# A PSUM bank chosen for every product, and new orders of all engines, in an attention and slot-mixture kernel

## The chip, the cores and the metric

The kernel runs on one core of a Trainium2 chip. Five engines work side by side, each through its own queue of instructions in order: TensorE (PE; its weight loads are shown as PEld), VectorE (DVE), ScalarE (ACT), GpSimd (POOL) and SyncE (SP, which here only starts transfers). They wait for each other by semaphores. Time is device time of one execution in microseconds (us), from several runs.

## What is computed

The input x has 32 batches of 256 tokens with 128 features. Each batch goes through two layers, each with a layer norm on both sides and a residual. Cut to what matters (16 heads of 8 features; 8 experts of 64 slots, so 512 slots; 512 hidden features):

```python
def _L0_attn_ref(x, ...):                   # a sum over the sequence in place of a softmax
    q = exp(x @ Wq.T + bq); k = exp(x @ Wk.T + bk); v = x @ Wv.T + bv     # per head
    kv = cumsum(k[:, :, :, None] * v[:, :, None, :], axis=1)
    num = einsum('zsD,zsDd->zsd', q, kv)
    den = sum(q * cumsum(k, axis=1), axis=-1)
    return (num / den) @ Wo.T + bo
def _L0_ffn_ref(x, ...):                    # soft mixture over slots
    xn, se = rms_norm(x, gamma_x), rms_norm(slot_embeds, gamma_slot)
    logits = einsum('bsd,etd->bset', xn, se)
    slots = einsum('bsd,bset->betd', xn, softmax(logits, axis=1))         # over the tokens
    processed = gelu(slots @ w1) @ w2
    return einsum('bnd,bsn->bsd', processed, softmax(logits, over all slots))
x = x + layernorm(attn(layernorm(x)))
x = x + layernorm(ffn(layernorm(x)))
```

## The kernel before

All weights stay in SBUF. A batch's 256 tokens are two per partition (c = 0 and 1), and all 32 batches go through one software pipeline: a `step(s)` of each engine's queue works on several batches at once, at different depths. Most operations are small functions, such as `gather_slots(n)`, and each engine's order of calls is written out by hand: `first_steps()` for the first batches, then `step(s)` in a loop, then `last_steps()`. Nothing else sets the order of the work.

The way of one batch n is this. DVE takes statistics of x (`x_statistics`), POOL raises the variance to the power -1/2 (`x_rstd_of`), DVE normalises (`x_normalise`, result xh), PE transposes (`x_transpose`), ACT and DVE make a high and a low part of it (`xT_high`, `xT_low`). `project(n, c)` gives q, k and v of one token parity; ACT evicts them to E (`qk_evict` with exp, `v_evict`). SP shifts E's odd tokens by one partition with a transfer (`shift_odd`, into prev). POOL forms outer products of k and v (`outer_even`, `outer_odd`, 1,024 columns each), adds them (`pair_sum`) and splits the sum (`sums_high` writes kv_hi, `sums_low` writes kv_lo). PE sums over partitions with a triangle (`cumulate(n, k)`, three thirds k), DVE multiplies each third with q (`multiply(n, k)`), reduces (`attention_sums`) and divides (`attention`). PE transposes att, ACT copies it (`attT_copy`), and `attention_out` gives y. ACT squares y, POOL gives its inverse root (`y_rstd_of`, y_rs), and DVE adds y to x (`first_residual`, x1).

Then the mixture: ACT squares x1, POOL gives x1_rs (`x1_rstd_of`), DVE normalises (`x1_normalise`, xn), PE transposes, ACT and DVE split. `logits(n)` fills the two banks of LB. DVE takes two maxima (`slot_maxima`, `part_maxima`), ACT takes four exponentials (`dispatch_exp`, disp_t), and DVE scales them (`dispatch_scale`). PE transposes disp_t (`dispatch_transpose`), ACT copies each half to disp (`dispatch_copy`), and PE gathers the slots (`gather_slots`). Their high and low parts are slT_hi and slT_lo. `hidden(n, f)` makes the four quarters of the hidden layer, ACT takes the Gelu of each, `process(n, h)` multiplies by w2, and `mixture(n)` mixes with comb. ACT squares the result, POOL gives o_rs, and DVE adds it to x1 (`second_residual`, res), which SP stores. ACT loads one table for Exp and one for Gelu in each step.

A product with both operands split is three matmuls (`three`). PSUM has eight banks of 512 columns. They are named in pairs: WB serves the projections, all transposes of x, att, xn and the maxima, the cumulative sums, y, and the attention sums ND; LA the dispatch transposes and the mixture; HB the gathered slots, the hidden quarters (f % 2) and process; LB the logits. At the start PE also runs matmuls with no use (`spin`), 130 in all, in places where it would wait.

Of the kernel before, what the change touches and what calls it, by code (L numbers as in the profile page):

```python
# [5 lines left out]
def attention_and_slot_mixture(  # L6
# [45 lines left out]
    with ctx:  # L52
# [6 lines left out]
        def sem(name):  # L59
# [97 lines left out]
        s_wT, s_woT, s_wop, s_wu, s_sesum, s_senorm, s_kappa = (  # L157
            sem("s_" + n) for n in ("wT", "woT", "wop", "wu", "sesum", "senorm", "kappa"))
        s_gxs, s_sefloor, s_sehi, s_wqkvhi, s_wqkv, s_w1hi, s_wo_t = (
            sem("s_" + n) for n in ("gxs", "sefloor", "sehi", "wqkvhi", "wqkv", "w1hi", "wo_t"))  # L160
        s_w2 = sem("s_w2")
# [14 lines left out]
        xT_lo_ready, qk_exp, kv_even, kv_odd, kv_den, kv_built = (  # L176
            sem("s_" + n) for n in ("xTlo", "qkexp", "kve", "kvo", "kvd", "kv"))
        kv_hi_ready, kv_lo_ready, qk_own_ready, own_den, own_ready, own_added = (
            sem("s_" + n) for n in ("kvhi", "kvlo", "qkown", "ownden", "own", "ownadd"))
        summed, den_ready, att_ready, att_T, attT_ready, wo_done = (  # L180
            sem("s_" + n) for n in ("summed", "deninv", "att", "attTp", "attT", "wo"))
        y_var, y_rstd, x1_ready, x1_var, x1_floor, x1_rstd = (
            sem("s_" + n) for n in ("yve", "yrs", "x1", "x1ve", "x1fl", "x1rs"))
        xn_ready, xnT_done, xnT_hi_ready, xnT_lo_ready, lb_done, part_ready = (
            sem("s_" + n) for n in ("xn", "xnT", "xnThi", "xnTlo", "lb", "part"))
# [34 lines left out]
        def _(sp):  # L220
# [9 lines left out]
            @each_batch  # L230
            def shift_odd(n):
                sp.wait_ge(qk_exp, n + 1)
# [19 lines left out]
            def step(s):  # L252
                load(s)
                store(s - 8)
                shift_odd(s - 1)
# [8 lines left out]
        def _(pool):  # L264
# [17 lines left out]
            def x_rstd_of(n):  # L282
                pool.wait_ge(x_stats, n + 1)
                if n == 2:
                    after(pool, xh_ready, n - 1)
# [9 lines left out]
            def wo_order():  # L295
                pool.wait_ge(s_woload, 16)
                pool.tensor_copy(wo_p[:, :].rearrange("p (d h) -> p d h", d=HD),
                                 w_in[:, 3, :].rearrange("p (h d) -> p d h", d=HD)).then_inc(s_wop, 1)

            def slot_norms():  # L300
                pool.wait_ge(s_sesum, 1)
# [6 lines left out]
            def sums_high(n):  # L308
                after(pool, cum_done[2], n - 1)
                if n == 1:  # L310
                    pool.wait_ge(kv_den, n + 1)
# [10 lines left out]
            def own_value(n):  # L322
                pool.wait_ge(own_den, n + 1)
# [30 lines left out]
            def outer_even(n):  # L354
                if n == 0:
                    pool.wait_ge(qk_exp, n + 1)
# [13 lines left out]
            @each_batch  # L370
            def pair_keys(n):
                u = n % 2
                pool.tensor_tensor(kv[:, KVF:FEAT], E[u][:, 0, DIM:2 * DIM], prev[u][:, 0:DIM], ALU.add)\
                    .then_inc(kv_den, 1)
# [10 lines left out]
            def first_steps():  # L385
                wo_order()
                slot_norms()
# [4 lines left out]
                outer_odd(1)  # L392
                outer_even(1)
                pair_sum(1)
                x_negative(1)
                pair_keys(1)
                own_value(0)
                sums_high(1)
                sums_low(1)
                own_product(1)  # L400
                x_rstd_of(3)
                y_rstd_of(0)
                outer_odd(2)
                x1_rstd_of(0)
                x_negative(2)
                own_value(1)
                outer_even(2)
                pair_keys(2)
                pair_sum(2)
                own_product(2)  # L410
                sums_high(2)
                sums_low(2)
                y_rstd_of(1)
                x_rstd_of(4)
                outer_odd(3)
                x1_rstd_of(1)
                x_negative(4)
                x_negative(3)
                own_value(2)
                outer_even(3)  # L420
                pair_keys(3)
                pair_sum(3)
                own_product(3)
                sums_high(3)
                x_rstd_of(5)
                sums_low(3)
                y_rstd_of(2)
                outer_odd(4)
                x1_rstd_of(2)
                own_value(3)  # L430
                outer_even(4)
                pair_keys(4)
                pair_sum(4)
                own_product(4)
                sums_high(4)
                x_rstd_of(6)
# [1139 lines left out]
```

## Time and profile before

| | us |
|---|---|
| median of 3 runs (lowest to highest) | 620.16 (617.2 to 620.59) |
| the profiled execution | 618.45 |
| its span, from the first instruction to the last | 616.7 |
| PE, PEld busy | 586.3, 498.7 |
| DVE, ACT, POOL busy | 488.9, 448.1, 501.2 |

The span is what the rows below divide up; the profiled execution's own time has 1.75 us around it. A busy time of 95% on PE does not mean 95% of its peak, since the ends of matmuls are modelled and overlap. From start to start is the safer distance.

### The profile page before, as it was taken

The numbers are of one execution on the slowest core, as the hardware profiler recorded it, in microseconds if no ns is written. First come the engines' busy times: TensorE is split into PE (matmuls) and PEld (weight loads), VectorE is DVE, ScalarE is ACT, GpSimd is POOL, SyncE is SP. The second block draws the span as 40 slices with busy tenths as digits, with TensorE's granted clock in tenths as the row PEclk, the third lists the DMA queues.
The fourth block names the chain that finished last, engine by engine and source line by source line (L and its number), as shares of the span: only waits on it lengthen the run. The fifth ranks groups of instructions, "written<-read, shape, count | busy, mean of one in ns | idle before, by whom it ended". The sixth has DMA issues, their size and how long they took to land.

```text
span 616.7 us, 10792 instructions
## 1 busy us (share of the span) xinstructions
PE 586.3 (95%) x3884; PEld 498.7 (81%) x3884; DVE 488.9 (79%) x922; ACT 448.1 (73%) x1213; POOL 501.2 (81%) x493
## 2 busy tenths in 40 slices
PE   7988999999999999999999999999999999999986
PEld 7976888888888888888888888888888888887775
DVE  6778788888888888888888888888888888877630
ACT  4046787877777878777778787777787877777763
POOL 5589898898888988988889899888898898985100
PEclk9999999999999999999999999999999999999999
DMA  4000000000000000000000000010000000000000
GB/s 111 10 19 19 18 17 10 27 18 25 27 27 27 25 10 27 19 27 26 27 28 27 10 25 18 27 27 25 27 27 11 26 17 27 19 27 9 10 10 17
DMA packets 16825, 14.29 MB, mean 23 GB/s; under 512 B 2850, under 2 KB 16644, under 8 KB 16772
## 3 DMA queue, kind: packets, MB, share of 16 engines
q1 hardware_dynamic: 14708, 12.76, 6.9%
q10 hardware_dynamic: 2064, 0.86, 0.5%
q8 instruction: 30, 0.49, 0.4%
q14 instruction: 23, 0.19, 0.1%
HBM read 5.25 MB, written 4.19 MB: 15 GB/s over the span
## 4 chain that ended last, share of the span: by engine, by line
PE 45%; ACT 34%; POOL 8%; DVE 4%; issue 3%; DMA 0%; DVEq 0%; POOLq 0%; SPq 0%
PE HB L984 10%; ACT disp_t L660 9%; PE LA L1004 9%; POOL y_rs L333 7%; PE HB L849 5%; ACT disp L550 5%; PE HB L851 5%; PE HB L850 5%; ACT L558 4%; ACT x_sq L595 4%; DVE x L1351 3%; PE WB L849 3%; ACT y_sq L587 3%; ACT E L610 2%; ACT hid L570 2%
## 5 line engine op out<-in xcount | busy, mean ns | idle before, releaser
L993 PE MATMUL HB<-w_c,hid 128*128 128x128 f32 x1024 | 124.9, 275 | 2.3 <-ACT hid L570 2.3
L993 PEld LDWEIGHTS HB<-w_c,hid 128*128 128x128 f32 x1024 | 121.1, 192 | 3.6 <-ACT hid L570 3.6
L1311 DVE TENSOR_TENSOR prod<-WB,E 128x768 f32<-128x768 f32 x96 | 88.3, 949 | 3.6 <-PE WB L937 3.6
L570 ACT ACTIVATE hid<-HB 128x512 f32<-128x512 f32 x128 | 76.2, 598 | 14.0 <-PE HB L851 5.8
L1329 DVE TENSOR_REDUCE WB<-prod 128x288 f32<-128x2304 f32 x32 | 82.0, 2561 | 1.1
L318 POOL TENSOR_TENSOR kv_lo<-kv,kv_hi 128x1152 fp32r<-128x1152 f32 x31 | 81.8, 2638 | 0.2
L984 PE MATMUL HB<-disp,xn 128*128 128x512 f32 x128 | 63.3, 617 | 12.7 <-ACT disp L550 12.6
L379 POOL TENSOR_TENSOR kv<-kv,kv_prev 128x1024 f32<-128x1024 f32 x31 | 74.6, 2405 | 0.1
L204 POOL TENSOR_TENSOR kv_prev<-prev 128x1024 f32<-128x1024 f32 x31 | 66.5, 2145 | 9.4 <-DMA prev<-E 9.3
L204 POOL TENSOR_TENSOR kv<-E 128x1024 f32<-128x1024 f32 x32 | 68.5, 2140 | 1.4 <-ACT E L610 1.3
L333 POOL TENSOR_TENSOR y_rs<-y_ve,minus_half 128x2 f32<-128x2 f32 x32 | 45.0, 1407 | 29.4 <-ACT y_sq L587 29.4
L1004 PE MATMUL LA<-proc,comb 128*128 128x129 f32 x512 | 62.5, 274 | 0.8 <-ACT proc L550 0.8
L1004 PEld LDWEIGHTS LA<-proc,comb 128*128 128x128 f32 x512 | 59.9, 191 | 1.9 <-issue 1.9
L660 ACT ACTIVATE disp_t<-LB,neg_max 128x256 f32<-128x256 f32 x128 | 59.0, 486 | 0.0
L849 PE MATMUL HB<-slT_hi,w_hi 128*128 128x512 f32 x128 | 56.2, 439 | 0.5 <-ACT hid L570 0.3
L984 PEld LDWEIGHTS HB<-disp,xn 128*128 128x128 f32 x128 | 21.8, 189 | 37.5 <-ACT disp L550 22.0
L850 PE MATMUL HB<-slT_lo,w_hi 128*128 128x512 f32 x128 | 50.6, 395 | 0.0
L851 PE MATMUL HB<-slT_hi,w_lo 128*128 128x512 f32 x128 | 50.5, 394 | 0.0
L550 ACT ACTIVATE proc<-HB 128x512 f32<-128x512 f32 x32 | 19.1, 598 | 38.3 <-PE HB L993 38.3
L345 POOL TENSOR_TENSOR o_rs<-o_ve,minus_half 128x2 f32<-128x2 f32 x32 | 22.3, 697 | 30.3 <-ACT o_sq L604 30.3
L550 ACT ACTIVATE slT_hi<-HB 128x512 fp32r<-128x512 f32 x32 | 19.1, 597 | 30.9 <-PE HB L984 30.9
L554 ACT ACT_TABLE_LOAD x32 | 41.1, 1283 | 0.6
(138 smaller groups left out, 1595.6 us busy)
## 6 DMA issues: line engine op xcount, KB each, us to landing
X<-in_L_attn_x_dram SPq DMA_DIRECT2D x32, 128.0 KB, 2.1
out_dram<-res SPq DMA_DIRECT2D x32, 128.0 KB, 2.0
prev<-E SPq DMA_DIRECT2D x32, 112.0 KB, 2.2
w_in<-in_L_ffn_w_dram ACTq DMA_DIRECT2D x2, 256.0 KB, 4.5
prev<-E SPq DMA_DIRECT2D x32, 15.0 KB, 2.0
se_in<-n_L_ffn_slot_embeds_dram ACTq DMA_DIRECT2D x1, 256.0 KB, 3.6
w_in<-in_L_attn_Wq_dram SPq DMA_DIRECT2D x1, 64.0 KB, 2.4
w_in<-in_L_attn_Wk_dram SPq DMA_DIRECT2D x1, 64.0 KB, 2.1
```

The lines of the kernel that those rows point to most:

```text
L204: return eng.tensor_tensor(dst.rearrange("p (d h e) -> p d h e", d=HD, h=NH), k.rearrange("p (o h e) -> p o h e", o=1, h=NH).broadcast_to( ...
L318: pool.tensor_tensor(kv_lo[:, :], kv[:, :], kv_hi[:, :].bitcast(F32), ALU.subtract)\
L333: pool.tensor_tensor(y_rs[:, :], y_ve[:, :], minus_half[:, 0:NC], ALU.pow).then_inc(y_rstd, 1)
L570: act.activation(hid[:, f, :], HB[:, f % 2, :], ACT.Gelu).then_inc(gelu_ready[f], 1)
L660: last = act.activation(disp_t[:, j, :], LBv[:, j, :], ACT.Exp, bias=neg_max[:, j:j + 1], accum_out=disp_sum[:, j:j + 1])
L849: pe.matmul(dst, a_hi, b_hi, start=start, stop=False, skip_group_check=True)
L850: pe.matmul(dst, a_hi, b_lo, start=False, stop=False, skip_group_check=True)
L984: last = pe.matmul(HB[:, 0, :], xn[n % 2][:, c, :], disp[:, c, :], start=(c == 0), stop=(c == NC - 1))
L993: last = pe.matmul(PR[:, j, :], hid[:, f, j * P:(j + 1) * P], w2_c[:, f, :], start=(f == 0), stop=(f == FJ - 1))
L1004: last = pe.matmul(OB[:, c, :], comb[n % 2][:, j, c * P:(c + 1) * P], proc[:, j, 0:YW], start=(j == 0), stop=(j == SJ - 1))
L1311: dve.tensor_tensor(prod[u][:, :, d0 * DIM:d1 * DIM].rearrange("p c (d f) -> p c d f", d=g), WB[:, k % 2, 0:g * DIM].rearrange("p (o d f) ...
L1329: dve.tensor_reduce(ND.rearrange("p c f h -> p c (f h)"), prod[n % 2][:, :, :].rearrange("p c (f e) -> p c f e", e=HD), AX.X, ALU.add).the ...
```

## The change

Every product now has a bank of its own choice out of one tensor `banks` of eight. The mixture OB uses one bank (its two halves side by side) where it used two. The four hidden quarters lie in four banks. What must not overlap is guarded by new waits. The orders of all engines are new, in the loop, the start and the end; PE's spins are 70 in place of 130. `step(s)` is also cut at another place of the pipeline on most engines, so that the numbers of its calls differ where the order of the work does not.

```diff
-        WB = pb("WB", [P, 2, 512])
-        LA = pb("LA", [P, 2, 512])
-        LB = pb("LB", [P, 2, 512])
-        HB = pb("HB", [P, 2, 512])
...
+        banks = pb("banks", [P, 8, 512])
+        WB = banks[:, 0:2, :]
+        LB = banks[:, 2:4, :]
...
+        XT = banks[:, 6, 0:SEQ]
+        XN = banks[:, 2, 0:SEQ]
+        PT = banks[:, 5, 0:SEQ]
+        CU = [banks[:, 5, 0:DU * DIM], banks[:, 7, 0:DU * DIM], banks[:, 4, 0:DU * DIM]]
+        ND = banks[:, 5, 0:NC * (HD + 1) * NH].rearrange("p (c f h) -> p c f h", c=NC, h=NH)
+        AT = banks[:, 7, 0:SEQ]
+        YO = banks[:, 7, 0:NC * YW]
+        YB = YO.rearrange("p (c d) -> p c d", d=YW)
+        DT = [banks[:, 0, :], banks[:, 1, :]]
+        SL = banks[:, 0, :]
+        HP = [banks[:, 3, :], banks[:, 0, :], banks[:, 7, :], banks[:, 1, :]]
+        PR = banks[:, 6, :].rearrange("p (j d) -> p j d", d=DIM)
+        OB = banks[:, 4, 0:NC * YW].rearrange("p (c d) -> p c d", d=YW)
```

The waits on PE that the prediction speaks of:

```diff
             def hidden(n, f):
...
+                elif f == 1:
                     pe.wait_ge(slT_lo_ready, n + 1)
-                elif f == 1:
-                    if n in (28, 29):
-                        pe.wait_ge(slT_lo_ready, n + 1)
-                elif f == 2:
-                    pe.wait_ge(gelu_ready[0], n + 1)
-                elif f == 3:
-                    pe.wait_ge(gelu_ready[1], n + 1)
...
             def project(n, c):
...
-                    after(pe, attT_ready, n - 2)
+                    after(pe, gelu_ready[3], n - 4)
...
             def logits(n):
+                after(pe, gelu_ready[0], n - 1)
                 pe.wait_ge(xnT_lo_ready, n + 1)
...
             def gather_slots(n):
-                pe.wait_ge(disp_ready[1], n + 1)
...
+                pe.wait_ge(disp_ready[0], n + 1)
```

SP, where the shift moves ahead of the store, and one line of POOL's and one of DVE's loop:

```diff
             def step(s):
                 load(s)
+                shift_odd(s - 1)
                 store(s - 8)
-                shift_odd(s - 1)
...
-                sums_low(s - 2)
+                sums_low(s - 1)
...
-                attention_sums(s - 3)
+                attention_sums(s - 2)
```

PE's queue in the loop from the dispatch transposes (`LA<-ident,disp_t`) to the gather of slots (`disp,xn`); the matmuls with tri are the thirds of the cumulative sum, the one with neg_ident subtracts the maxima. Before:

```order
L963 MATMUL LA<-ident,disp_t 128x128 [waits s_dscale]
L963 MATMUL LA<-ident,disp_t 128x128 x3
L936 MATMUL WB<-kv_hi,tri 128x384 [waits s_kvlo]
L937 MATMUL WB<-kv_lo,tri 128x384
L963 MATMUL LA<-ident,disp_t 128x128 x4
L936 MATMUL WB<-kv_hi,tri 128x384 [waits s_x1]
L937 MATMUL WB<-kv_lo,tri 128x384
L972 MATMUL LB<-neg_ident,tok_max 128x2x128 [waits s_dexp,s_tok]
L972 MATMUL LB<-neg_ident,tok_max 128x2x128 x3
L936 MATMUL WB<-kv_hi,tri 128x384 [waits s_prod0]
L937 MATMUL WB<-kv_lo,tri 128x384
L984 MATMUL HB<-disp,xn1 128x512 [waits s_disp1]
```

The same place in the changed kernel:

```order
L865 MATMUL banks<-kv_hi,tri 128x384 [waits s_res,s_kvlo]
L866 MATMUL banks<-kv_lo,tri 128x384
L865 MATMUL banks<-kv_hi,tri 128x384
L866 MATMUL banks<-kv_lo,tri 128x384
L891 MATMUL banks<-ident,disp_t 128x128 [waits s_dscale]
L891 MATMUL banks<-ident,disp_t 128x128 x7
L902 MATMUL banks<-neg_ident,tok_max 128x2x128 x4
L865 MATMUL banks<-kv_hi,tri 128x384 [waits s_x1]
L866 MATMUL banks<-kv_lo,tri 128x384
L809 MATMUL banks<-ident,xh 128x128 [waits s_procs,s_xh]
L809 MATMUL banks<-ident,xh 128x128
L912 MATMUL banks<-disp,xn0 128x512 [waits s_disp0]
```

Two thirds of the cumulative sum moved ahead of the dispatch transposes, which stand together now; the third that waits for x1 and the transposes of x stand ahead of the gather.

ACT's queue in the loop, from the squares of y to the slots' eviction (slT_hi). Before:

```order
L587 ACTIVATE y_sq,y_ve<-WB 128x129
L550 ACTIVATE proc<-HB 128x4x128 [waits s_proc1]
L595 ACTIVATE x1_sq,x1_v<-x1_2,neg_m1 128x128 [waits s_x1]
L595 ACTIVATE x1_sq,x1_v<-x1_2,neg_m1 128x128
L550 ACTIVATE disp<-LA 128x512 [waits s_dispT0]
L550 ACTIVATE disp<-LA 128x512 [waits s_dispT1]
L678 ACTIVATE comb0<-LB 128x512 [waits s_lbs]
L678 ACTIVATE comb0<-LB 128x512 [waits s_comb0]
L550 ACTIVATE slT_hi<-HB 128x512 [waits s_slT]
```

The same place in the changed kernel:

```order
L504 ACTIVATE y_sq,y_ve<-banks 128x129
L467 ACTIVATE proc<-banks 128x4x128 [waits s_proc1]
L467 ACTIVATE disp<-banks 128x512 [waits s_dispT1]
L467 ACTIVATE disp<-banks 128x512 [waits s_dispT0]
L512 ACTIVATE x1_sq,x1_v<-x1_2,neg_m1 128x128 [waits s_x1]
L512 ACTIVATE x1_sq,x1_v<-x1_2,neg_m1 128x128
L602 ACTIVATE comb0<-banks 128x512 [waits s_lbs]
L492 ACTIVATE xT_hi<-banks 128x256 [waits s_xT]
L467 ACTIVATE slT_hi<-banks 128x512 [waits s_slT]
```

The copies of disp moved ahead of the squares of x1, and the eviction of x's transposes came in ahead of slT_hi.

POOL's queue in the loop, from own_product (qk_own) to kv_lo and y_rs. Before, y_rs (line 333) is the instruction behind these:

```order
L350 TENSOR_TENSOR qk_own<-E1 128x128
L313 CAST kv_hi<-kv 128x1152 [waits s_kv,s_cum2]
L286 TENSOR_SCALAR x_ve<-x_mv3 128x2 [waits s_xst]
L288 TENSOR_TENSOR x_rs<-x_ve,minus_half 128x2 [waits s_xve]
L345 TENSOR_TENSOR o_rs<-o_ve,minus_half 128x2 [waits s_ove]
L318 TENSOR_TENSOR kv_lo<-kv,kv_hi 128x1152 [waits s_kvhi]
```

The same place in the changed kernel:

```order
L357 TENSOR_TENSOR qk_own<-E1 128x128
L319 CAST kv_hi<-kv 128x1152 [waits s_kv,s_cum1]
L352 TENSOR_TENSOR o_rs<-o_ve,minus_half 128x2 [waits s_ove]
L324 TENSOR_TENSOR kv_lo<-kv,kv_hi 128x1152 [waits s_kvhi]
L293 TENSOR_SCALAR x_ve<-x_mv3 128x2 [waits s_xst]
L295 TENSOR_TENSOR x_rs<-x_ve,minus_half 128x2 [waits s_xve]
L340 TENSOR_TENSOR y_rs<-y_ve,minus_half 128x2 [waits s_yve]
```

x_rs moved behind kv_lo, directly ahead of y_rs.

## Rows read from the trace of the kernel before

**Rows 1.** The page, part 1: busy time and share of each engine.

```profile
PE 586.3 (95%) x3884; PEld 498.7 (81%) x3884; DVE 488.9 (79%) x922; ACT 448.1 (73%) x1213; POOL 501.2 (81%) x493
```

**Rows 2.** One step by windows: length, busy of each engine, clock, DMA share, GB/s.

```profile
core 0: us, PE busy (x) PEld busy (x) DVE busy (x) ACT busy (x) POOL busy (x), PEclk, DMA share, GB/s
319.66:337.28 17.62, 17.17 (x115) 14.57 (x115) 14.84 (x29) 13.75 (x38) 15.81 (x16) 1.00 0.08 24
```

**Rows 3.** The waits: who waited for whom, us in total, times, longest.

```profile
PEld HB L984 <- ACT disp L550: 22.0, 30, 1.0
...
PEld WB L849 <- ACT attT L550: 10.6, 28, 0.5
...
POOL kv_prev L204 <- DMA prev<-E: 9.3, 6, 6.3
```

**Rows 4.** The chain that ended last, in order of time: start, us, what.

```profile
91.58 1.98 PE HB L984 x4
...
549.71 1.98 PE HB L984 x4
```

**Rows 5.** The timeline of PE in one step: start, us, what.

```profile
303.05 1.99 PE L984 MATMUL HB<-disp,xn 128*128 128x512 f32 x4 [0.39 <-ACT disp L550]
...
306.80 0.48 PE L849 MATMUL HB<-slT_hi,w_hi 128*128 128x512 f32 x1
...
308.43 0.50 PE L849 MATMUL HB<-slT_hi,w_hi 128*128 128x512 f32 x1
...
309.93 0.28 PE L849 MATMUL LB<-xnT_hi,se_hi 128*128 128x256 f32 x1
...
313.11 1.95 PE L993 MATMUL HB<-w_c,hid 128*128 128x128 f32 x16
...
317.52 0.66 PE L963 MATMUL LA<-ident,disp_t 128*128 128x128 f32 x4
...
320.66 0.70 PE L984 MATMUL HB<-disp,xn 128*128 128x512 f32 x1 [0.40 <-ACT disp L550]
```

**Rows 6.** The timelines of DVE, ACT and POOL in the same step.

```profile
305.70 0.69 DVE L1238 TENSOR_TENSOR slT_lo<-HB,slT_hi 128x512 fp32r<-128x512 f32 x1 [0.32 <-ACT slT_hi L550]
...
307.42 2.56 DVE L1329 TENSOR_REDUCE WB<-prod 128x288 f32<-128x2304 f32 x1
...
316.24 1.23 DVE L1389 TENSOR_TENSOR disp_t<-disp_t,disp_inv 128x1024 f32<-128x1024 f32 x1
318.13 0.61 DVE L1351 SCALAR_TENSOR_TENSOR x<-WB,y_rs,X 128x128 f32<-128x128 f32 x2 [0.66 <-POOL y_rs L333]
318.65 1.81 DVE L1311 TENSOR_TENSOR prod<-WB,E 128x768 f32<-128x768 f32 x2
320.38 0.60 DVE L1217 TENSOR_SCALAR xh<-X,x_mv,x_rs 128x128 f32<-128x128 f32 x2
...
316.59 1.43 POOL L333 TENSOR_TENSOR y_rs<-y_ve,minus_half 128x2 f32<-128x2 f32 x1 [0.74 <-ACT y_sq L587]
...
319.56 1.05 ACT L550 ACTIVATE disp<-LA 128x512 f32<-128x512 f32 x2
```

**Rows 7.** The page, part 5: groups with count, busy, mean ns, idle before.

```profile
L318 POOL TENSOR_TENSOR kv_lo<-kv,kv_hi 128x1152 fp32r<-128x1152 f32 x31 | 81.8, 2638 | 0.2
...
L333 POOL TENSOR_TENSOR y_rs<-y_ve,minus_half 128x2 f32<-128x2 f32 x32 | 45.0, 1407 | 29.4 <-ACT y_sq L587 29.4
...
L345 POOL TENSOR_TENSOR o_rs<-o_ve,minus_half 128x2 f32<-128x2 f32 x32 | 22.3, 697 | 30.3 <-ACT o_sq L604 30.3
```

**Rows 8.** The timeline of PE in the last but one step of the tail.

```profile
580.64 1.09 PE L963 MATMUL LA<-ident,disp_t 128*128 128x128 f32 x8
582.57 1.96 PE L984 MATMUL HB<-disp,xn 128*128 128x512 f32 x4 [0.83 <-ACT disp L550]
```

**Rows 9.** The timelines of DVE and POOL near 12.5 us.

```profile
12.52 2.18 DVE L1261 CAST b_hi<-b_row 33x129 fp32r<-33x129 f32 x1
...
12.49 2.13 POOL L204 TENSOR_TENSOR kv<-E 128x1024 f32<-128x1024 f32 x1 [1.32 <-ACT E L610]
```

**Rows 10.** The spins (line 830) by a window: length, PE and PEld busy, clock, DMA.

```profile
18.72:58.90 40.18, 21.80 (x178) 21.25 (x178) 1.00 0.06 18
```

More of the change, by code:

```diff
@@ L406, in first_steps @@
[L406 to L436, printed above, removed]
-                o_rstd_of(0)
-                sums_low(4)
-                y_rstd_of(3)
@@ L579, in attT_copy @@
                 act.wait_ge(att_T, n + 1)
-                copy(attT[:, :], WB[:, 1, 0:SEQ]).then_inc(attT_ready, 1)
+                copy(attT[:, :], AT).then_inc(attT_ready, 1)
             @each_batch
@@ new lines, in step, with last_steps @@
+                xT_low(s)
+                attention(s - 2)
+                slot_maxima(s - 3)
+                part_maxima(s - 3)
+            def last_steps():
+                x_statistics(31)
+                token_maxima(27)
+                second_residual(25)
+                dispatch_scale(27)
+                x_normalise(31)
+                first_residual(28)
+                multiply(29, 2)
+                multiply(29, 1)
+                multiply(29, 0)
+                x1_normalise(28)
+                own_sum(29)
+                slT_low(27)
+                attention_sums(29)
+                xnT_low(28)
+                xT_low(31)
+                attention(29)
+                slot_maxima(28)
+                part_maxima(28)
+                token_maxima(28)
+                second_residual(26)
+                dispatch_scale(28)
+                multiply(30, 2)
+                first_residual(29)
+                own_sum(30)
+                multiply(30, 1)
+                multiply(30, 0)
+                x1_normalise(29)
+                slT_low(28)
+                attention_sums(30)
+                xnT_low(29)
+                attention(30)
+                slot_maxima(29)
+                part_maxima(29)
+                token_maxima(29)
+                second_residual(27)
+                dispatch_scale(29)
+                own_sum(31)
+                first_residual(30)
+                multiply(31, 2)
+                multiply(31, 1)
+                multiply(31, 0)
+                x1_normalise(30)
+                slT_low(29)
+                attention_sums(31)
+                xnT_low(30)
+                attention(31)
+                part_maxima(30)
+                slot_maxima(30)
+                token_maxima(30)
+                second_residual(28)
+                dispatch_scale(30)
+                first_residual(31)
+                x1_normalise(31)
+                slT_low(30)
+                xnT_low(31)
+                slot_maxima(31)
+                part_maxima(31)
+                token_maxima(31)
+                second_residual(29)
+                dispatch_scale(31)
+                slT_low(31)
+                second_residual(30)
+                second_residual(31)
```

711 lines of the change are left out of this document (295 added, 416 removed).

## Prediction

> **What bounds the kernel now.** I read the page's head first [rows 1]: TensorE (PE) is busy for 95% of the span, the other engines 73 to 81%. So PE is either the bound or is released by a loop that is almost as long. The window of one step [rows 2] says how near: 17.17 us of PE busy time in 17.62 us, at a granted clock of 1.00. Modelled ends overlap, so busy time hides small stalls; the distance from start to start has to be used. The list of waits [rows 3] then names what PE's weight loads wait for: the ACT copy of disp ahead of the gather of slots (22.0 us over 30 steps), and the copy of attT in the second projection (10.6 us).
>
> The chain that ended last [rows 4] shows a period: the gather (line 984) starts at 91.58 and, 26 steps later, at 549.71, so (549.71 - 91.58) / 26 = 17.62 us a step. With 91.6 us ahead of that and 67.0 behind it this is the 616.7 us span. The same chain runs through POOL's y_rs of line 333 in each step.
>
> One step on PE from gather to gather [rows 5]: 3.75 (gather, transposes of xn, mixture), 1.63 and 1.50 (two pairs of hidden products, x's transposes behind the first), 3.18 (logits, att, projections), 4.41 (the halves of process, with part and attention-out between them), 3.14 (dispatch transposes, cumulative sums, maxima subtracted, idle). Sum 17.61.
>
> **How the loop closes.** Write G for a gather's start and D for the end of DVE's scaling of disp_t. From G to the logits: 309.93 - 303.05 = 6.88. From there to D: 316.24 + 1.23 = 317.47, so 7.54. From D to the next G at 320.66: 3.19 [rows 5, 6]. That last piece is the loose one. y_rs of POOL takes 1.43 us where o_rs, the same operation on the same shape, has a mean of 0.70 [rows 7]; it started at 316.59, while DVE scaled disp_t from 316.24 to 317.47, and ended 0.55 us behind it. x1 follows at 318.13 to 318.74, ACT squares x1, and only then, at 319.56, copies disp; the gather starts 0.05 us after the two copies. So the gather waits for x1, which it does not use.
>
> **The change, part by part.** *(a) Banks.* Hidden products 2 and 3 had to wait for the Gelus of products 0 and 1; the second projection waited for attT's copy out of its bank. With a bank for each product both waits go. After a wait the next matmul comes about 0.1 us late, since its weights weren't loaded under the one ahead; I take 0.13 off the hidden stretch (308.43 shows one such start; 3.13 with x's transposes of 0.15 becomes 2.85). Logits to projections loses 0.41: the wait for attT is 10.6 us over 28 steps, 0.38 each [rows 3], and 0.03 is taken for the restart. Process is taken to lose 0.06 in its restart at 313.11. *(b) Order at the gather.* ACT now copies both halves of disp before it squares x1. PE does both dispatch transposes first, then subtract, the last cumulative sum and x's transposes. At the gather the weights wait 22.0 us over 30 steps, 0.73 each [rows 3]; part of that lies under the last cumulative sum, and I count 0.55 of the 3.14 as lost. All four together: 1.15 us, and PE alone would need 17.61 - 1.15 = **16.46 us** a step; that is the floor.
>
> *(c) Does a loop take PE's place?* G to logits is now 3.75 + 2.85 = 6.60, logits to D stays 7.54 (DVE's two maxima, ACT's four exponentials, DVE's scaling stand in the same order; ACT evicts q, k, v and attT ahead of them as before). D to G has three candidates. Copies: the tail has exactly this form, eight transposes at 580.64, gather at 582.57 [rows 8], 1.93 plus 0.05: period 6.60 + 7.54 + 1.98 = 16.12, under the floor. x1, if POOL's x_rs is ready at D: x_normalise 0.52 (the like residual takes that from start to start, 318.13 to 318.65), own_sum 0.20 (my estimate: 128 columns against the 2,304 of the attention sums' 2.56), residual 0.60 [rows 6], then the cumulative sum that waits for x1 and x's transposes, together 0.6, and 0.2 for two semaphores: 2.15, period 16.29, also under it. But x_rs moves: on POOL it stood ahead of kv_lo and now stands behind it, directly ahead of y_rs. By my count it comes up while DVE scales disp_t, the place where y_rs stood before. Then both are held: x_rs ends at D + 0.55, y_rs at D + 1.25, DVE normalises x until D + 1.2, own_sum 1.4, residual 2.0, and G is D + 2.61: period **16.75 us**. I take this one: y_rs shows the hold in the mean of its 32 runs (1407 ns [rows 7]), and DVE, which waited 0.66 for y_rs, now works on x_normalise there.
>
> The Trainium skill (SBUF — State Buffer, section Who interferes with whom) says that VectorE and GpSimd share one pair of ports as an exclusive lock, taken by a VectorE instruction with two SBUF inputs or in a 2-port mode, and that the later one blocks fully. The trace agrees: 1.43 against 0.70 us. By this rule the loss can as well fall on DVE, which is a rival below; without any lock the sum would be the floor's 16.46.
>
> Other moved steps: attention_sums now precedes xnT_low. In before, slT_low starts at 305.70, 2.65 after the gather, and takes 0.69; with the sums' 2.56 at 307.42 [rows 6] and 0.4 for xnT_low that is 6.3 after G, logits at 6.6: covered by 0.3. If that cover is gone, each tenth over costs a tenth a step. Gelus 1, 0, 3, 2 with their table load end under the logits and projections. On SP the shift of E is queued ahead of the store now, so a store no longer delays it; POOL waited for that transfer only 6 times, 9.3 us in all [rows 3], and so it is priced at nothing in the steps.
>
> *(d) The ends.* At the start the 130 warming matmuls become 70, bo's centring leaves the place ahead of the second projection, where one cast took 2.18 us beside a POOL product begun 0.03 us earlier [rows 9], and comes back behind attention(0). POOL gets slot_norms and an own_product ahead of its second sums. I cannot add this up closely; bounds are 0 (the cast is only moved) and 4 (the wait of PE there is all gained). I take 2, nearer to the steps' saving of 0.86 in two early steps. At the end four hidden products without restarts: 0 to 2, taken as 1.
>
> **Sum.** 26 x (17.62 - 16.75) = 22.6, plus 2 and 1: 25.6. The profiled execution took 618.45 us (span 616.7), so 592.9. The median of the three runs, 620.16, lies 1.7 above that execution; half of it added: **594 us**.
>
> **Rivals.**
> 1. *PE at its floor.* x_rs comes up before DVE's scaling, or y_rs overlaps nothing. 26 x 1.16 + 3 = 33: 585 us. For it: all loops I find are at or under 16.5 then. Against: POOL's place behind kv_lo. 15%.
> 2. *POOL couples to DVE.* POOL needs 15.81 - 0.73 = 15.1 us a step [rows 2, 6]. From y_rs's end at D + 1.25 kv_lo ends at about D + 14.8 to 15.2 and the scaling starts at D + 15.5. If POOL loses 0.5 to 0.8 more on the way (each lost port contest costs up to an operation), kv_lo, 2.6 us long [rows 7], holds the scaling itself. Period near 17.2: 26 x 0.42 + 3 = 14: 605 us. 20%.
> 3. *DVE's normalise of xn is held (the other side).* It is reached at D + 2.0 + 3 x 0.87 = D + 4.6, when POOL ends x1_rs; outer_even, 2.1 us on POOL [rows 9], starts at D + 5.3. If DVE comes 0.7 later, it is held to D + 7.4, slT_low ends at 8.6, and hidden starts 2.3 late: 19.05 a step, 652 us in every step, 623 when it strikes every other one. It decides from a mean hold of 0.87 us a step. For it: the cast of 2.18 us [rows 9] is such a hold on DVE. Against: a margin of 0.7 us, and POOL is slowed by the same things as DVE. 13%, all beyond 0.5% slower.
> 4. *The change does nothing in the loop*: a wait of the same length elsewhere (xnT_low late, gelu 0 late for the logits, which it now guards). The steps stay within 0.1 of 17.6: 616 to 622 us. 7%.
> 5. *A colder PE at the start.* Spins fill 21.80 us of the 40.18 us from 18.72 to 58.90 [rows 10], at full clock; after the 37 spins ahead of the first cumulative sum none stands there now. If the granted clock falls to its lower level, 1.2 GHz, the roughly 15 us of other matmuls there double, a third of it on the path as I judge by the idle gaps: 5 us over the forecast, 599 us. 5%. The Trainium skill (TensorE: Matmul & The Clock Gate, section What's actually happening) speaks for it: idle stretches bring the half clock; no row before shows it, since the spins cover them.
>
> **Numbers.** The forecast case, 16.6 to 16.95 a step, has 40% and spans 589 to 599 us. 583 to 613 leaves out the slower 13%, the seven of rival 4, hardly more. 0.5% is about what a measurement of this kernel can tell from no change (617 to 623 us): faster 0.80 (forecast, 1, 2, 5), same 0.07, slower 0.13.
>
> **What would show it.** Gathers 16.6 to 16.9 us apart; ACT's disp copies directly behind the transposes, x1's squares behind them; PE's remaining wait of 0.1 to 0.4 us in front of the cumulative sum for x1 rather than at the gather; x_rs or y_rs above 1.2 us in place of 0.70; hidden products 0.23 apart throughout. Wrong would be: a DVE normalise of 1.5 us or more in each step (rival 3), a scaling longer than 1.23 us (rival 2), PE idle in front of the logits (rival 4), a granted clock under 1 between 20 and 60 us (rival 5).

## The result and the profile after

| | us |
|---|---|
| before, median of 4 runs | 619.61 (617.2 to 620.59) |
| after, median of 4 runs | 689.88 (688.12 to 691.51) |
| ratio | 1.114, 95% interval 1.1095 to 1.1185 |
| after, the profiled execution and its span | 691.51, 689.8 |

The changed kernel is 11% slower, where 594 us was forecast. Runs over 1.5% above the fastest of their own kernel, two in experiment 3 and one in experiment 4, are left out of that experiment's ratio. The page of the changed kernel: first the busy time, then the shares of the chain that ended last, then groups (busy, mean ns, idle before).

```profile
PE 583.6 (85%) x3764; PEld 496.1 (72%) x3764; DVE 562.5 (82%) x922; ACT 446.4 (65%) x1213; POOL 502.8 (73%) x493
...
DVE prod L1231 8%; DMA out_dram<-res 7%; DVE xn L1277 7%; DVE xh L1134 7%; PE banks L787 6%; PE banks L789 5%; SPq L244 5%; PE banks L788 5%; ACT L475 5%; DVE disp_t L1309 3%; PE banks L912 3%; PE banks L935 3%; ACT o_sq L522 3%; ACT hid L487 2%; DVE res L1324 2%
...
L213 POOL TENSOR_TENSOR kv_prev<-prev 128x1024 f32<-128x1024 f32 x31 | 86.3, 2785 | 3.8 <-DMA prev<-E 3.8
...
L1324 DVE SCALAR_TENSOR_TENSOR res<-banks,o_rs,x 128x128 f32<-128x128 f32 x64 | 19.5, 346 | 57.0 <-DMA out_dram<-res 45.5
...
L1277 DVE TENSOR_SCALAR xn<-x,x_mv,x_rs 128x128 f32<-128x128 f32 x64 | 60.1, 979 | 2.5 <-POOL x_rs L347 2.5
...
L1134 DVE TENSOR_SCALAR xh<-X,x_mv,x_rs 128x128 f32<-128x128 f32 x64 | 53.7, 879 | 3.0 <-POOL x_rs L295 3.0
```

PE is no longer nearly full (95% in [rows 1]). Two things are new in the chain. One is SP's shift (line 244) with the transfer of the result out, `out_dram<-res`, 12% together. The other is the two normalises of DVE, xn and xh, of nearly 1 us each. DVE's residual `res` waits 45.5 us for that transfer, 1.8 us a time in 25 steps:

```profile
DVE res L1324 <- DMA out_dram<-res: 45.5, 25, 2.9
```

When does it begin? The timeline of DVE at the start of the loop (start, us) shows res, the scaling and the normalise of x in steps two to four:

```profile
86.95 1.22 DVE L1309 TENSOR_TENSOR disp_t<-disp_t,disp_inv 128x1024 f32<-128x1024 f32 x1
...
103.83 1.22 DVE L1309 TENSOR_TENSOR disp_t<-disp_t,disp_inv 128x1024 f32<-128x1024 f32 x1
105.92 0.60 DVE L1134 TENSOR_SCALAR xh<-X,x_mv,x_rs 128x128 f32<-128x128 f32 x2 [0.87 <-POOL x_rs L295]
121.53 0.61 DVE L1324 SCALAR_TENSOR_TENSOR res<-banks,o_rs,x 128x128 f32<-128x128 f32 x2 [1.67 <-DMA out_dram<-res]
122.26 1.23 DVE L1309 TENSOR_TENSOR disp_t<-disp_t,disp_inv 128x1024 f32<-128x1024 f32 x1
123.40 2.41 DVE L1134 TENSOR_SCALAR xh<-X,x_mv,x_rs 128x128 f32<-128x128 f32 x2
```

From 86.95 to 103.83 a step takes 16.88 us and has the forecast's form: DVE waits 0.87 us for x_rs behind the scaling. The residual of the third batch, at 121.53, is the first that needs a buffer back, and from there on steps take about 20.6 us. One such step, first ACT's eviction of v to E, then SP, then DVE, then POOL:

```profile
283.04 0.38 ACT L467 ACTIVATE E<-banks 128x256 f32<-128x256 f32 x1
283.44 1.43 SPq L244 DMA_DIRECT2D prev<-E  x2
284.92 0.55 SPq L254 DMA_DIRECT2D out_dram<-res  x1
```

```profile
284.77 0.42 DVE L1301 TENSOR_REDUCE tok_max<-banks 128x2 fp32r<-128x256 f32 x1 [0.24 <-PE banks L838]
286.88 0.61 DVE L1324 SCALAR_TENSOR_TENSOR res<-banks,o_rs,x 128x128 f32<-128x128 f32 x2 [1.69 <-DMA out_dram<-res]
...
287.61 1.22 DVE L1309 TENSOR_TENSOR disp_t<-disp_t,disp_inv 128x1024 f32<-128x1024 f32 x1
288.75 2.41 DVE L1134 TENSOR_SCALAR xh<-X,x_mv,x_rs 128x128 f32<-128x128 f32 x2
...
294.39 2.48 DVE L1277 TENSOR_SCALAR xn<-x,x_mv,x_rs 128x128 f32<-128x128 f32 x2
```

```profile
286.96 0.70 POOL L340 TENSOR_TENSOR y_rs<-y_ve,minus_half 128x2 f32<-128x2 f32 x1
287.63 3.19 POOL L213 TENSOR_TENSOR kv_prev<-prev 128x1024 f32<-128x1024 f32 x1
292.88 0.23 POOL L345 TENSOR_SCALAR x_vf<-x_v 128x2 f32<-128x2 f32 x1 [2.05 <-ACT x_sq L512]
...
294.66 2.13 POOL L213 TENSOR_TENSOR kv<-E 128x1024 f32<-128x1024 f32 x1
```

The store of batch s - 8 stands in SP's queue behind the shift of batch s - 1, which waits for this step's v to be evicted. The store's data have been ready for more than a step, since it is the result of two steps earlier that DVE waits to have stored. It is issued only at 284.92, and DVE, which needs its buffer, is free at 285.19 and starts at 286.88. DVE's scaling is then 1.7 us late, while POOL is not. x_rs ends ahead of it and y_rs 0.05 us behind its start, both unheld, and POOL's long product kv_prev lies beside the scaling: the product takes 3.19 us in place of 2.14, and DVE's next instruction, the normalise of x, ends only behind it (2.41 in place of 0.60). The same comes again at 294.39 with xn and outer_even. Over the 25 steps kv_prev holds the normalise of x in 19 and, where it began ahead of the scaling or with it, the scaling itself in the other 6 (2.06 to 3.22 us).

### The profile page after: what moved, and what is told of

The parts are those of the page before. It is cut to its first block, busy times and chain, and to the rows that moved or that the text cites. A ratio compares the mean times of both kernels' runs of the same rounds, so it can differ in the third digit from the quotient of the medians.

```text
span 689.8 us, 10635 instructions
## 1 busy us (share of the span) xinstructions
PE 583.6 (85%) x3764; PEld 496.1 (72%) x3764; DVE 562.5 (82%) x922; ACT 446.4 (65%) x1213; POOL 502.8 (73%) x493
## 4 chain that ended last, share of the span: by engine, by line
DVE 33%; PE 29%; ACT 15%; DMA 8%; issue 5%; SPq 5%; POOL 4%; POOLq 0%; DVEq 0%; ACTq 0%
DVE prod L1231 8%; DMA out_dram<-res 7%; DVE xn L1277 7%; DVE xh L1134 7%; PE banks L787 6%; PE banks L789 5%; SPq L244 5%; PE banks L788 5%; ACT L475 5%; DVE disp_t L1309 3%; PE banks L912 3%; PE banks L935 3%; ACT o_sq L522 3%; ACT hid L487 2%; DVE res L1324 2%
## 5 line engine op out<-in xcount | busy, mean ns | idle before, releaser
L922 PE MATMUL banks<-w_c,hid 128*128 128x128 f32 x1024 | 124.7, 276 | 1.4 <-ACT hid L487 1.4
L922 PEld LDWEIGHTS banks<-w_c,hid 128*128 128x128 f32 x1024 | 119.3, 192 | 2.2 <-ACT hid L487 2.2
L487 ACT ACTIVATE hid<-banks 128x512 f32<-128x512 f32 x128 | 76.9, 601 | 41.1 <-PE banks L789 36.5
L1231 DVE TENSOR_TENSOR prod<-banks,E 128x768 f32<-128x768 f32 x96 | 86.2, 944 | 4.8 <-PE banks L866 4.6
L1247 DVE TENSOR_REDUCE banks<-prod 128x288 f32<-128x2304 f32 x32 | 81.5, 2547 | 0.0
L935 PEld LDWEIGHTS banks<-proc,comb 128*128 128x128 f32 x512 | 62.1, 191 | 15.8 <-issue 15.8
L1324 DVE SCALAR_TENSOR_TENSOR res<-banks,o_rs,x 128x128 f32<-128x128 f32 x64 | 19.5, 346 | 57.0 <-DMA out_dram<-res 45.5
L935 PE MATMUL banks<-proc,comb 128*128 128x129 f32 x512 | 62.4, 275 | 0.8 <-ACT proc L467 0.8
L912 PE MATMUL banks<-disp,xn 128*128 128x512 f32 x128 | 62.0, 608 | 1.0 <-ACT disp L467 1.0
L584 ACT ACTIVATE disp_t<-banks,neg_max 128x256 f32<-128x256 f32 x128 | 58.9, 472 | 5.2 <-DVE part_max L1290 5.2
L1277 DVE TENSOR_SCALAR xn<-x,x_mv,x_rs 128x128 f32<-128x128 f32 x64 | 60.1, 979 | 2.5 <-POOL x_rs L347 2.5
```

Of the source, the lines that this page charges most:

```text
L487: act.activation(hid[:, f, :], HP[f], ACT.Gelu).then_inc(gelu_ready[f], 1)
L912: last = pe.matmul(SL, xn[n % 2][:, c, :], disp[:, c, :], start=(c == 0), stop=(c == NC - 1))
L922: last = pe.matmul(PR[:, j, :], hid[:, f, j * P:(j + 1) * P], w2_c[:, f, :], start=(f == 0), stop=(f == FJ - 1))
L935: last = pe.matmul(OB[:, c, :], comb[n % 2][:, j, c * P:(c + 1) * P], proc[:, j, 0:YW], start=(j == 0), stop=(j == SJ - 1))
L1231: dve.tensor_tensor(prod[u][:, :, d0 * DIM:d1 * DIM].rearrange("p c (d f) -> p c d f", d=g), CU[k].rearrange("p (o d f) -> p o d f", o=1, ...
L1247: dve.tensor_reduce(ND.rearrange("p c f h -> p c (f h)"), prod[n % 2][:, :, :].rearrange("p c (f e) -> p c f e", e=HD), AX.X, ALU.add).the ...
```

## The experiments

Every change to a kernel is shown against the changed kernel, or against the kernel before where its label begins with b. A ratio is always to the kernel before, run beside it.

**1. The store ahead of the shift again, everything else as changed.**

```diff
             def step(s):
                 load(s)
-                shift_odd(s - 1)
                 store(s - 8)
+                shift_odd(s - 1)
```

> The changed kernel with one thing undone: SP queues the store of a batch ahead of the shift of E again. Theory S (the late store is the trigger): in the changed kernel DVE waits about 1.7 us a step for the store's landing before it writes res; this delays the scaling of disp_t, so x_rs and y_rs of POOL get past it, outer_odd starts with the scaling and then holds DVE's normalise of x, and outer_even holds that of xn. With the store first all of it goes, the steps are 16.9 us as the changed kernel has them from 86 to 106 us, and the time is 595 to 605 us. Theory H (the holds between DVE and POOL come from the new orders by themselves): only the wait of 1.4 to 1.7 us in 25 steps goes, 645 to 655 us, and the normalises stay at 2.4 us.

Measured: 597.85 us, ratio 0.966 (0.9635 to 0.9685). Two lines of SP's order are worth 92 us. One step of this kernel on DVE:

```profile
288.58 1.22 DVE L1309 TENSOR_TENSOR disp_t<-disp_t,disp_inv 128x1024 f32<-128x1024 f32 x1
290.67 0.60 DVE L1134 TENSOR_SCALAR xh<-X,x_mv,x_rs 128x128 f32<-128x128 f32 x2 [0.87 <-POOL x_rs L295]
...
305.47 1.23 DVE L1309 TENSOR_TENSOR disp_t<-disp_t,disp_inv 128x1024 f32<-128x1024 f32 x1
```

and on POOL, from kv_lo to the product kv_prev:

```profile
285.87 2.63 POOL L324 TENSOR_TENSOR kv_lo<-kv,kv_hi 128x1152 fp32r<-128x1152 f32 x1
288.59 1.27 POOL L293 TENSOR_SCALAR x_ve<-x_mv 128x2 f32<-128x2 f32 x1
289.94 0.69 POOL L295 TENSOR_TENSOR x_rs<-x_ve,minus_half 128x2 f32<-128x2 f32 x1
290.61 0.71 POOL L340 TENSOR_TENSOR y_rs<-y_ve,minus_half 128x2 f32<-128x2 f32 x1
291.27 2.14 POOL L213 TENSOR_TENSOR kv_prev<-prev 128x1024 f32<-128x1024 f32 x1
```

The step is 305.47 - 288.58 = 16.89 us (16.75 was forecast), with x_ve held for the scaling's whole length, then x_rs, then y_rs. Nothing of the store's wait is left, and the normalises are short (DVE's groups in this kernel):

```profile
L1277 DVE TENSOR_SCALAR xn<-x,x_mv,x_rs 128x128 f32<-128x128 f32 x64 | 23.0, 399 | 2.5 <-POOL x_rs L347 2.5
L1134 DVE TENSOR_SCALAR xh<-X,x_mv,x_rs 128x128 f32<-128x128 f32 x64 | 21.3, 376 | 23.8 <-POOL x_rs L295 23.8
```

**2. The order of SP as changed, but three buffers for res.** The late store stays; nobody waits for it.

```diff
-        res = [sb(f"res{u}", [P, NC, DIM]) for u in range(2)]
+        res = [sb(f"res{u}", [P, NC, DIM]) for u in range(3)]
...
-                loaded(dve, stored, n - 2)
+                loaded(dve, stored, n - 3)
```

> The changed kernel with three buffers for res in place of two, and SP's order as the change has it, so the store is as late as before but nobody waits for it. Theory S expects what it expects of the store put first, 595 to 605 us with steps near 16.9 us; theory H 645 to 655 us. If this one is slow and the store put first is fast, the lateness of the store hurts in another way than by the buffer.

Measured: 596.78 us, ratio 0.9646 (0.9627 to 0.9666), with the same step of 16.89. So it is the buffer's wait that costs. The store may be late.

**3. The two lines swapped in the kernel before.**

```diff
             def step(s):
                 load(s)
+                shift_odd(s - 1)
                 store(s - 8)
-                shift_odd(s - 1)
```

> The kernel before with one part of the change alone: on SP the shift of E goes ahead of the store. In the kernel before, the shift is issued from 314.20 to 315.63 and the store would land near 317.7, while DVE writes res at 313.83. Theory S: DVE waits up to 3.9 us a step for it, part of it in waits that it has anyway (0.87 and 0.30 us), so a step takes 19.5 to 21 us and the time is 665 to 700 us. Theory H: the order on SP is only a small part, under 640 us.

Measured: 718.45 us, ratio 1.1521 (1.1449 to 1.1592). By the ratio, which is that of the two faster runs (709.6 and 716.49), the one swap makes the old kernel slower by 94 us as well; the 665 to 700 us expected were too few. From the waits and DVE's timeline of its longest run (720.89 us):

```profile
DVE res L1404 <- DMA out_dram<-res: 102.5, 25, 5.3
```

```profile
302.45 0.61 DVE L1404 SCALAR_TENSOR_TENSOR res<-LA,o_rs,x 128x128 f32<-128x128 f32 x2 [3.70 <-DMA out_dram<-res]
```

The wait is 4.1 us a step here against 1.8. So the loss needs neither the banks nor the orders of the other engines: 94 us here and 92 in the changed kernel cannot be told apart, given the spread of 7 us between the two faster runs.

**4. How much is the wait, and how much the holds?** Both normalises of DVE are given an accumulator output, a form that also changes the values it writes; the rest is the changed kernel.

```diff
-                                             x_rs[:, c:c + 1], ALU.subtract, ALU.mult)
+                                             x_rs[:, c:c + 1], ALU.subtract, ALU.mult, accum_out=acc_sink[:, c:c + 1])
```

> The changed kernel with both normalises of DVE (of x and of xn) in the form that also writes a sum over the columns to a small unused tile. By the Trainium skill (SBUF — State Buffer, Who interferes with whom) this form of tensor_scalar takes no 2-port mode and does not contend with GpSimd. If POOL's outer products are what holds the normalises, each falls from 2.4 us to about 1 us (two instructions at half the rate and two reads of the sum), the wait for the store stays at 1.7 us, and a step takes 17.3 to 18.5 us: 605 to 635 us. If the 2.4 us have another cause, they stay and the time is 685 us or more.

Measured: 631.49 us, ratio 1.0172 (1.0118 to 1.0225). The wait for the store is as before, and the normalises are short in spite of POOL's product beside them:

```profile
DVE res L1325 <- DMA out_dram<-res: 45.5, 25, 2.8
```

```profile
L1135 DVE TENSOR_SCALAR_CACHE_REDUCE xh<-X,x_mv,x_rs 128x128 f32<-128x128 f32 x64 | 23.3, 400 | 3.0 <-POOL x_rs L296 3.0
L1278 DVE TENSOR_SCALAR_CACHE_REDUCE xn<-x,x_mv,x_rs 128x128 f32<-128x128 f32 x64 | 23.2, 399 | 2.5 <-POOL x_rs L348 2.5
```

Of the 92 us between the changed kernel and experiment 1, the holds of the normalises are 689.88 - 630.91 = 59 (630.91 is the median of the three faster runs) and 33 are left. These 33 are not all the wait's own. The scaling in three steps of this kernel:

```profile
192.02 2.35 DVE L1310 TENSOR_TENSOR disp_t<-disp_t,disp_inv 128x1024 f32<-128x1024 f32 x1
...
271.53 1.22 DVE L1310 TENSOR_TENSOR disp_t<-disp_t,disp_inv 128x1024 f32<-128x1024 f32 x1
289.04 1.22 DVE L1310 TENSOR_TENSOR disp_t<-disp_t,disp_inv 128x1024 f32<-128x1024 f32 x1
```

Where DVE has nothing held, in 16 of the 25 steps, a step takes 17.51 us or so, only 0.6 more than experiment 1's 16.89 although the wait is 1.7: DVE's wait of 0.87 us for x_rs behind the scaling is gone. Six scalings are held by kv_prev (2.15 to 3.02 us), and the nine longer steps around these and at the first wait bring the rest. So the wait alone is worth about 25 x 0.6 = 16 us, and what is left, about 17, falls in those nine steps. The Trainium skill (SBUF — State Buffer, section Who interferes with whom) says that `tensor_scalar` can take the ports shared with GpSimd, but not in the form that also writes out its accumulator. The trace agrees: mean 979 and 879 ns in the one form, 399 and 400 in the other, beside the same POOL queue.

**5. x_rs out of the scaling's way.** From here on the store is first. The statistics of x move ahead of the slot maxima on DVE, and x_rs ahead of o_rs and kv_lo on POOL.

```diff
             def step(s):                      # POOL
-                x_rstd_of(s)
+                if s <= 5:
+                    x_rstd_of(s)
...
                 sums_high(s - 1)
+                if s >= 5:
+                    x_rstd_of(s + 1)
                 o_rstd_of(s - 5)
                 sums_low(s - 1)
...
             def step(s):                      # DVE
-                x_statistics(s)
...
                 attention(s - 2)
+                x_statistics(s + 1)
                 slot_maxima(s - 3)
```

> The store first, and besides the two statistics of x stand ahead of slot_maxima on DVE (where it idles 0.71 us) and x_rs ahead of o_rs and kv_lo on POOL, from batch 6 on. Hold theory (the forecast's, rival 1 its other side): a step takes 16.89 us because x_ve waits behind the scaling (1.27 us in place of 0.19) and x_rs and y_rs come after it; with x_rs up early DVE normalises x at the scaling's end, x1 comes 0.7 to 0.9 us sooner, and the step falls to PE's 16.45 to 16.6: 587 to 591 us. Rival, POOL couples to DVE: POOL idles only 0.28 us in a step, so kv_lo now starts about 0.6 us later, ends behind the start of the scaling and holds it; the step stays at 16.8 to 17.2 us, 596 to 605 us, with a scaling or a wait ahead of it longer than 1.23 us.

Measured: 586.39 us, ratio 0.9471 (0.9456 to 0.9486), faster than both kernels. DVE and then POOL in this kernel:

```profile
283.24 1.77 DVE L1311 TENSOR_TENSOR disp_t<-disp_t,disp_inv 128x1024 f32<-128x1024 f32 x1
...
299.75 1.80 DVE L1311 TENSOR_TENSOR disp_t<-disp_t,disp_inv 128x1024 f32<-128x1024 f32 x1
301.47 0.59 DVE L1136 TENSOR_SCALAR xh<-X,x_mv,x_rs 128x128 f32<-128x128 f32 x2
```

```profile
297.83 2.64 POOL L324 TENSOR_TENSOR kv_lo<-kv,kv_hi 128x1152 fp32r<-128x1152 f32 x1
300.42 1.68 POOL L340 TENSOR_TENSOR y_rs<-y_ve,minus_half 128x2 f32<-128x2 f32 x1
```

and PE's weight load of the dispatch transposes, behind the scaling:

```profile
301.60 0.86 PEld L893 LDWEIGHTS banks<-ident,disp_t 128*128 128x128 f32 x8 [0.43 <-DVE disp_t L1311]
```

The step is 299.75 - 283.24 = 16.51 us. Both theories have their part. DVE no longer waits for x_rs. But kv_lo, now 0.8 us later against the scaling (it ended 0.08 us ahead of it and now ends 0.72 behind its start), holds it until 300.4, so that it takes 1.80 us in place of 1.23. That hold is on the path: the weights of the dispatch transposes wait 0.43 us for the scaling. y_rs in turn is held behind the scaling (1.68 us in place of 0.70). So the step is that of a loop through POOL and DVE, and not PE's floor, though it is only 0.05 us from the 16.46 forecast for that.

**6. The hidden quarters in two banks again**, with the waits of the kernel before.

```diff
-        HP = [banks[:, 3, :], banks[:, 0, :], banks[:, 7, :], banks[:, 1, :]]
+        HP = [banks[:, 7, :], banks[:, 1, :], banks[:, 7, :], banks[:, 1, :]]
...
...
+                elif f == 3:
+                    if n != 30:
+                        pe.wait_ge(gelu_ready[1], n + 1)
+                elif f == 2:
+                    pe.wait_ge(gelu_ready[0], n + 1)
...
```

> The store first, but the four hidden quarters in two banks again (quarters 0 and 2 in bank 7, 1 and 3 in bank 1), with the two waits of before for the Gelus. This takes the banks' part of the change back. The forecast priced the restarts at 0.13 us a step for a PE that is the bound. With the step set by the loop through POOL (16.89 against PE's 16.46) the hidden stretch still lies in it (gather to logits), so: 0.1 to 0.25 us a step, 600 to 604 us. Rival: PE has 0.45 us of slack ahead of the last cumulative sum and takes it from there: 597.5 to 598.5 us, no difference.

Measured: 608.13 us, ratio 0.9825 (0.9806 to 0.9844), 10.3 more than with four banks. The scaling of this kernel, a step apart:

```profile
294.52 1.23 DVE L1316 TENSOR_TENSOR disp_t<-disp_t,disp_inv 128x1024 f32<-128x1024 f32 x1
...
311.75 1.23 DVE L1316 TENSOR_TENSOR disp_t<-disp_t,disp_inv 128x1024 f32<-128x1024 f32 x1
```

17.23 us, so 0.34 a step, more than the 0.1 to 0.25 expected. PE waits 0.45 us ahead of the last cumulative sum in experiment 1 (at 292.08), but that slack is at another place of the loop; the restarts lie between gather and logits and lengthen the step.

**7 and 8. The warming matmuls.** The windows of experiment 1 and of the next kernel, 30 to 40 us (length, busy of PE, PEld, DVE, ACT and POOL, then the granted clock, DMA share, GB/s):

```profile
30.00:40.00 10.00, 5.83 (x18) 4.82 (x19) 8.96 (x24) 2.19 (x10) 7.26 (x9) 0.55 0.05 14
```

```profile
30.00:40.00 10.00, 10.00 (x88) 9.96 (x87) 7.90 (x21) 1.15 (x3) 5.46 (x7) 1.00 0.05 15
```

The second is experiment 1 with spins in PE's gaps:

```diff
+                warm(34)
                 project(2, 1)
...
+                warm(20)
                 attention_out(0)
...
+                warm(6)
                 cumulate(1, 1)
                 x_transpose(3)
+                warm(16)
                 xn_transpose(0)
+                warm(17)
                 logits(0)
```

> The changed kernel with the store ahead of the shift on SP, and 93 more warming matmuls (34, 20, 6, 16 and 17) in PE's five long gaps between 27 and 46 us, into bank 3, which is free there. With the store first alone the granted clock was 0.78 from 20 to 40 us and 0.71 from 40 to 60. Cold-clock theory: about 15 us of that stretch are other matmuls at the lower level, of which a third lies on the path; with the gaps filled the clock stays at 1.00 and the first gather comes 2 to 5 us earlier, 593 to 596 us in place of 597.9. Rival: the start is set by DVE and POOL (DVE busy 4.2 to 4.8 us in nearly every 5 us there), so the clock recovers and the time does not: 597 to 598 us.

Measured: 601.06 us, ratio 0.971 (0.9693 to 0.9727), slower than without them by 3.2 although the clock is full from 20 to 60 us. PE's timeline has the reason, the first spins and the first gather:

```profile
27.01 7.76 PE L770 MATMUL banks<-ident 128*128 128x128 f32 x68
...
60.83 1.97 PE L916 MATMUL banks<-disp,xn 128*128 128x512 f32 x4
```

34 of them are 68 records and 7.76 us. I had counted 0.11 us for each, and it is 0.23, so they overfilled the gap. With half of them (17, 10, 3, 8, 8):

> The kernel of a_sf_spins with half the warming matmuls: 17, 10, 3, 8 and 8 in the same five gaps. The run of a_sf_spins showed two records of 0.11 us for each, so 34 took 7.76 us in a gap of 3.85; PE itself had become late by 3.7 us. Cold-clock theory: with the gaps filled and not overfilled the granted clock stays at 1.00 and the first gather, at 57.06 us with the store first alone, comes at 52 to 56 us: 593 to 596.5 us. Rival, DVE and POOL set the start: the clock is full and the first gather stays at 56.5 to 57.5 us, 597 to 598.5 us.

Measured: 596.14 us, ratio 0.9639 (0.9613 to 0.9666). The interval overlaps that of experiment 1. In the profiled executions the clock is full from 20 to 50 us and the first gather comes at 55.87 in place of 57.06. The same spins upon experiment 5:

> The store first, x_rs and statistics early (586.4 us without spins) and the halved warming matmuls. Cold-clock theory: 581 to 585 us. Rival: 585.5 to 587 us.

Measured: 586.17 us, ratio 0.9476 (0.9453 to 0.9499), against 586.39 without: no difference. The full number of spins upon experiment 5,

> The store first, x_rs and the statistics early, and the warming matmuls, together. Hold and cold-clock theories: the sum of both, 583 to 588 us. If both rivals hold: 596 to 605 us. If only one of the two theories holds, this shows the gain of that one alone.

gave 590.76 us, ratio 0.954 (0.9525 to 0.9555), 4.4 more than without, for the same reason as above. Filling the gaps brings the first gather forward by 1.2 us in both pairs (from 57.06 to 55.87, and from 56.51 to 55.32 upon experiment 5), not by 5, and the medians by less than their intervals can tell. The spins may take back a part of what the clock gives. DVE is busy for 8.96 of the ten us in the first window above and POOL for 7.26, so I take these two to set the pace there; no run shows that by itself.

**9. x_rs early with SP's order as changed.**

> The changed kernel with x_rs and the statistics of x early, SP as the change has it (shift ahead of store). With the store first this edit took 11.5 us. Late-store theory: the wait of res for the transfer out (45.5 us) stands ahead of the scaling whatever POOL does; it puts DVE late against POOL, whose 2.1 us product then holds the normalise of xn. So both costs remain: 665 to 700 us. Rival, the holds come from POOL's order at the scaling: with x_rs early the normalises are 0.35 us each again and only the store's wait of about 34 us remains: 615 to 635 us.

Measured: 687.28 us, ratio 1.1107 (1.108 to 1.1134). An edit worth 11.5 us with the store first is worth under 3 here. From the waits and from DVE's groups:

```profile
DVE res L1326 <- DMA out_dram<-res: 43.8, 25, 2.4
```

```profile
L1311 DVE TENSOR_TENSOR disp_t<-disp_t,disp_inv 128x1024 f32<-128x1024 f32 x32 | 79.1, 2472 | 1.1
L1279 DVE TENSOR_SCALAR xn<-x,x_mv,x_rs 128x128 f32<-128x128 f32 x64 | 46.1, 760 | 2.5 <-POOL x_rs L347 2.5
L1136 DVE TENSOR_SCALAR xh<-X,x_mv,x_rs 128x128 f32<-128x128 f32 x64 | 21.0, 368 | 1.3 <-POOL x_rs L295 1.3
```

The hold has moved, from the normalise of x to the scaling in front of it (2.47 us in place of 1.23): DVE still comes 1.7 us late, so a POOL product, kv_prev, lies beside whichever instruction of DVE stands there. The normalise of xn is still held, in about every other step (mean 760 ns against 399 in experiment 1).

## Why the prediction was wrong, point by point

**The step that failed.** It is the last of the moved steps: "On SP the shift of E is queued ahead of the store now, so a store no longer delays it; POOL waited for that transfer only 6 times, 9.3 us in all [rows 3], and so it is priced at nothing in the steps." It asks what the moved shift gains and not what it does to the store now behind it: what the shift waits for, and who waits for the store. Undone by itself (experiment 1) the time is 597.85; done by itself (experiment 3) it costs 94 us. The place could be followed in the order of the queues. The shift waits for v of its batch, evicted behind the logits and the projections. The store's transfer takes 1.9 us from issue to landing. DVE's res, two batches on, stands ahead of the scaling, at the tightest place of the loop.

**How 1.7 us a step became 3.7.** Steps of 20.6 against 16.9 over 25 steps make 25 x 3.7 = 93 us. Experiment 4 splits it. Its undisturbed steps take 17.5: of the 3.7 us, 0.6 is the wait alone and 3.1 is DVE's two normalises held by POOL's products. In whole times it is 33 and 59, since even there POOL holds six scalings. Rival 3 had the second half as a mechanism, with its price (xn of 1.5 us or more, 652 us in every step) and its condition, DVE late by 0.7 us against POOL. I took the lateness to be an accident. With the wait of 1.7 us a POOL product holds DVE in all of the 25 steps. What I missed as well is that xh can be held in the same way, by kv_prev.

**Right, with the store first.** The forecast case, x_rs and y_rs both coming behind the scaling: 16.89 against 16.75, x_ve held 1.27 us, and DVE's wait 0.87. 26 x 0.14 = 3.6 us is what the term was off; the forecast's 594 stands against a measured 597.85. The piece from D to the gather was 2.95 us (289.80 to 292.75) where the sum had 2.61: it let x_rs end at D + 0.55, without the x_ve that stands ahead of it and is the one held, and x_rs ended at D + 0.83. It also left out the 0.2 for two semaphores that it counted for the other case (whose terms add up to 2.12, not 2.15). The rest of the loop was 0.2 shorter than taken. The ends gave 1.6 + 0.2 us where 2 + 1 were taken: the third gather at 89.98 in place of 91.58, and 66.8 us behind the 29th in place of 67.0.

**Near by luck.** Rival 1, x_rs ahead of the scaling with PE at its floor of 16.46, forecast 585, and experiment 5 gives 16.51 a step and 586.39. But in it PE waits for the held scaling, so the loop through POOL and DVE sets the step. PE stands still for about 0.27 us there (301.33 to 301.60), so it alone would need about 16.2 by this estimate, and the floor was too high.

The signs named for the orders are there: ACT's copies of disp directly behind the transposes, and the hidden products 0.23 us apart.

**The price of the banks.** The hidden stretch was given 0.13 us a step for the restarts. Experiment 6 puts them at 0.34 in the new orders; what they cost in the old ones no run shows. The direction was right.

**Rival 5.** The clock fell as it said, to 0.62 between 30 and 40 us and to 0.50 between 40 and 50 in the changed kernel, its lower level of 1.2 GHz, after idle times of PE of 3.14 and 3.60 us (ahead of 31.53 and 37.20). Its price of 5 us did not show: filling the gaps gave back 1.2 us at the first gather (experiment 8).

**Rival 2** (kv_lo holds the scaling) is seen in experiment 5, at 0.57 us a step. It lies on the path there, but the step had become short enough by then that the period is 16.51 and not the 17.2 that the rival gave.

## What to carry to other kernels

An issuing queue works in order, so a start of a transfer that waits must be priced for each transfer behind it: when it was ready, when it is now issued, who needs its buffer, and where that engine stands in the loop. A wait added on DVE ahead of a place where DVE and POOL just miss each other can cost more than its length, because the misses become holds; here 1.7 us of wait cost 3.7 a step, 0.6 by itself and 3.1 by the holds. One buffer more, or one line's place in a queue, was worth 92 us, against the 21 us that the change gains without it (experiment 1). And a step that comes out at the forecast floor is no proof of it: look whether the engine still waits.

## What the runs showed of the hardware

- A small and a large POOL instruction lose the same beside DVE's scaling (1.22 us): x_ve of two columns, started 0.01 us behind it, takes 1.27 us in place of 0.19; the product of 1,024 columns, started 0.02 us behind it, takes 3.19 in place of 2.14. So the later one loses nearly the length of the other, 1.08 and 1.05 us, whatever its own size.
- A normalise of 128 columns with an accumulator output takes 0.40 us, and 0.08 for the read of the accumulator, and is not held by a POOL product (experiment 4: from 290.18 to 290.91 inside kv_prev's 289.14 to 292.27). The plain form takes 0.38 to 0.40 in the mean if POOL leaves it alone; a pair takes 0.60 then, and 2.41 where POOL's product holds it.
- A warming matmul on fp32 data of 128 columns leaves two records and takes 0.23 us at the full clock (7.76 us for 34).
